# Second layer: output stored by GpSimd with indirect transfers instead of by SyncE

## The reference

```python
xn = layernorm(x)
# attention: a fast-weight recurrence over the leading axis (4 steps here), 16 heads of 64
h = norm(xn) * ln_w + ln_b
q, k, v, beta = split(h @ w_slow);  q, k = sum_norm(elu(q) + 1), sum_norm(elu(k) + 1)
W = 0
for t in range(4):
    W = W + (beta_t * (v_t - W k_t)) k_t^T
    out_t = W q_t
attn = xn + out @ w_out
# feed-forward: 8 experts, the best 2 of each row by softmax(xn @ Wg), their relu nets weighted and summed
x = x + attn + moe(xn)
```

## Time and profile before

| | |
|---|---|
| runs | 1483.12 us median of 2 (1481.14 to 1485.11) |
| the profiled execution, its own time | 1482.89 us |
| its span, first to last instruction | 1481.2 us |
| granted TensorE clock | 0.995 of full speed |
| busy, share of the span | PE 96%, DVE 85%, POOL 65%, ACT 62% |

### The profile page before, as it was taken

How to read it: one execution, slowest core, us unless ns; L and a number is a source line. 1 busy time by engine, 2 the same in 40 slices (tenths; PEclk the granted TensorE clock), 3 DMA queues, 4 the chain that set the end, 5 groups by cost and what they waited for, 6 DMA issues and landing times.

```text
span 1481.2 us, 27229 instructions
## 1 busy us (share of the span) xinstructions
PE 1417.2 (96%) x9282; PEld 914.2 (62%) x9282; DVE 1255.7 (85%) x1966; ACT 916.9 (62%) x1862; POOL 968.5 (65%) x756
## 2 busy tenths in 40 slices
PE   8989999999999999999999998889999999999998
PEld 6755556555555565565655555456667676776767
DVE  7587888788877888888888777479999999999997
ACT  3456666666666667666666675557665675657562
POOL 5144555546555456455555554549999999999895
PEclk9999999999999999999999999999999999999999
DMA  8059777877787778777777778400000000000000
GB/s 189 1 129 217 173 172 179 185 170 175 174 185 173 172 173 186 172 168 178 181 181 166 178 177 199 102 1 1 0 9 8 1 8 1 8 8 1 8 1 15
DMA packets 77140, 163.98 MB, mean 111 GB/s; under 512 B 31410, under 2 KB 43724, under 8 KB 77004
## 3 DMA queue, kind: packets, MB, share of 16 engines
q1 hardware_dynamic: 77004, 162.24, 47.5%
HBM read 9.08 MB, written 2.10 MB: 8 GB/s over the span
## 4 chain that ended last, share of the span: by engine, by line
PE 81%; DVE 7%; issue 5%; POOL 3%; ACT 2%; SPq 0%; DMA 0%; DVEq 0%; ACTq 0%; POOLq 0%
PE accum L1095 17%; PE both L1030 12%; PE misc L997 9%; PE both L2785 8%; PE flips_all L1030 5%; PE flips_all L2808 4%; PE flips_all L1119 4%; PE misc L1007 4%; PE flips_all L2797 3%; PE flips_all L2845 2%; PE accum L2797 2%; PE accum L2808 2%; ACT big L533 2%; PE flips_all L2831 1%; PE flips_all L968 1%
## 5 line engine op out<-in xcount | busy, mean ns | idle before, releaser
L452 POOL TENSOR_SCALAR big<-big,recip 128x384 f32<-128x384 f32 (+7 forms) x512 | 374.4, 745 | 430.5 <-DVE recip L704 430.5
L712 DVE STREAM_TRANSPOSE big<-big 128x896 f32<-128x896 f32 (+7 forms) x288 | 346.0, 1227 | 17.5 <-POOL big L452 16.8
L533 ACT ACTIVATE big<-both,neg_max 128x1024 f32<-128x1024 f32 (+3 forms) x256 | 243.1, 955 | 162.7 <-DVE neg_max L694 157.5
L1095 PE MATMUL accum<-across,v_sb 128*64 128x256 f32 (+1 forms) x2560 | 272.8, 364 | 22.2 <-issue 21.8
L1095 PEld LDWEIGHTS accum<-across,v_sb 128*64 128x64 f32 x2560 | 187.0, 138 | 137.9 <-issue 82.5
L694 DVE TENSOR_REDUCE neg_max<-both 128x1 f32<-128x1024 f32 (+3 forms) x256 | 248.3, 1011 | 7.6 <-PE both L1035 7.6
L1030 PE MATMUL both<-qk_sb 64*128 64x512 f32 (+3 forms) x1024 | 212.9, 532 | 13.1 <-issue 8.2
L533 ACT ACTIVATE big<-flips_all,neg_max 128x128 f32<-128x128 f32 (+3 forms) x256 | 131.6, 525 | 102.7 <-DMA across<-big 59.8
L2785 PE MATMUL both<-slow_sb,h_T 128*128 128x512 f32 x384 | 181.2, 599 | 7.9 <-DVE xnT L2298 4.4
L1594 POOL TENSOR_TENSOR prod<-xnT,qs 128x1024 f32<-128x1024 f32 (+3 forms) x32 | 180.2, 5638 | 11.1 <-DVE qs L2298 11.1
L1030 PEld LDWEIGHTS both<-qk_sb 64*128 64x128 f32 x1024 | 94.1, 186 | 117.9 <-issue 117.9
(11 more groups left out here) (224 smaller groups left out, 2404.9 us busy)
## 6 DMA issues: line engine op xcount, KB each, us to landing
across<-big SPq DMA_DIRECT2D x1024, 144.0 KB, 3.1
out<-x SPq DMA_DIRECT2D x8, 256.0 KB, 2.3
x<-in_L_attn_x SPq DMA_DIRECT2D x3, 512.0 KB, 5.5
slow_sb<-in_L_attn_w_slow SPq DMA_DIRECT2D x3, 512.0 KB, 7.1
w_qk<-in_L_attn_qkv_w SPq DMA_DIRECT2D x2, 512.0 KB, 6.3
xn<-in_L_ffn_W SPq DMA_DIRECT2D x1, 1024.0 KB
x<-in_L_attn_x SPq DMA_DIRECT2D x2, 256.0 KB, 3.0
qs<-in_L_attn_qkv_w SPq DMA_DIRECT2D x1, 512.0 KB, 6.0
```

The source lines that it names most:

```text
L452: pool.tensor_scalar(part, part, recip[:, u % 2, SLOTS.index(row), h:h + 1], 0.0, ALU.mult, ALU.add).then_inc(scaled, 1)
L533: last = act.activation(probs_of(row, h).rearrange("p b j k -> p j b k"), scores_of(row, h).rearrange("p (j b k) -> p j b k", b=MOVES, k=3 ...
L712: dve.transpose(part, part).then_inc(turned[group_of(row)], 1)
L1095: last = pe.matmul(dst, lhsT=values_of(u, j, h), rhs=keys_of(g, rows[n:n + 2], j, h), start=j == 0, stop=j == rows[n + 1])
```

## The change

GpSimd gets a function `store(t)`: with the same waits as SP had it issues four indirect transfers, one for each s, of 128 rows of 512 bytes each. The rows' numbers come from a table `index` that GpSimd makes once by `iota`, between `key_products(0, 2)` and `query_products(0, 2)`. The calls stand in GpSimd's written order: `store(0)` after `sums(2, 2)`, `store(1)` after `sums(3, 2)`, `store(2)` after `row3_high(4)`, `store(3)` after `row3_high(5)`, `store(4)` after `row2(6)`, and `store(5)`, `store(6)`, `store(7)` after its last instruction, `row2(7)`. SP only waits for the end.

```diff
+        index = sb("index", [P, B * ROWS], I32)
...
-        joined, stored = sem("joined"), sem("stored")
-        out_v = out.rearrange("s (t p) e -> t p s e", p=P)
+        joined, stored, index_made = sem("joined"), sem("stored"), sem("index_made")
+        out_v = out.rearrange("s n e -> (s n) e")
...
             last_move(UNITS - 1, 1)
-            for t in range(ROWS):
-                for k, use in latest(given, t, [("expert", e) for e in range(X)] + [("join",)]):
-                    sp.wait_ge(place_kept[k], use)
-                sp.dma_start(out_v[at_of(t)], rows_of(t)).then_inc(stored, 16)
-            sp.wait_ge(stored, 16 * ROWS)
+            sp.wait_ge(stored, 16 * ROWS * B)
...
+            def store(t):
+                if t == 0:
+                    pool.wait_ge(index_made, 1)
+                for k, use in latest(given, t, [("expert", e) for e in range(X)] + [("join",)]):
+                    pool.wait_ge(place_kept[k], use)
+                for s in range(B):
+                    at = ROWS * s + at_of(t)
+                    pool.indirect_dma_start(out_v, bass.IndirectOffsetOnAxis(ap=index[:, at:at + 1], axis=0), row_of(t, s), None
+                                            ).then_inc(stored, 16)
...
             pool.wait_ge(*all_added)
+            pool.iota(index[:], pattern=[[P, B * ROWS]], base=0, channel_multiplier=1).then_inc(index_made, 1)
             query_products(0, 2)
...
             sums(2, 2)
+            store(0)
             query_products(3, 0)
...
             sums(3, 2)
+            store(1)
             query_products(4, 0)
...
             row3_high(4)
+            store(2)
             query_products(5, 0)
...
             row3_high(5)
+            store(3)
             query_products(6, 0)
...
             row2(6)
+            store(4)
             query_products(7, 0)
...
             row2(7)
+            store(5)
+            store(6)
+            store(7)
```

## The result

The changed kernel takes 1513.6 us, the median of two runs (1513.01 to 1514.19), against 1483.12 before: 1.022 times, interval 1.018 to 1.026. Run again on another chip it took 1514.96 us (four runs) against 1481.33. The forecast was 1509.0 us. The kernel is slower beyond doubt; whether by more than 2% the interval leaves open. The direction and most of the size came out as worked out, by single steps that partly didn't.

What follows compares the result with a forecast made beforehand. PE, DVE and POOL were taken as full in the second layer, POOL just on time. Issues at 1.34 us each, 24c - 6.1 = 32.2 - 6.1 = +26.1 us on 1482.89, gave 1509.0 us; range 1487 to 1548.

Steps and rivals of the forecast that it cites:

- What bounds it: In the second layer PE, DVE and POOL are all full, and POOL is on time but not early.
- S: Time from the end of `sums(2, 2)` on POOL to the end of POOL's last product; forecast 21.8 us longer.
- The iota, the waits, SP's removal: Iota hidden in a POOL wait, counted 0; no store waits in its new place; removing SP's issues gives nothing before the end.
- C: Time from the end of POOL's last product to the start of DVE's last addition; forecast -0.25 us.
- T: Time from the end of DVE's last addition to the end of the span; forecast +4.6 us.
- c: Time one indirect transfer's issue holds POOL's queue; taken as 1.34 us, with ends 0.20 and 2.93.
- What is in hand: Lateness taken up after the first store: 2.81 and 2.23 us in POOL's idle times, 0.03 and 0.22 near the end; 5.3 us.
- The stores behind `row2(7)`: `store(5)` and `store(6)` after POOL's last instruction take 10.7 us and fit into the 14.4 us before the last addition ends.
- The tail: After the last addition, `store(7)` is bare: four issues, then the last 64 KB land; +4.6 us.
- Dear issue: Rival: each issue on POOL waits for a DVE instruction and costs 2.56 us; 1544.3 us; chance 0.25.
- Handed over: Rival: POOL passes each transfer on and goes on at once, 0.20 us an issue; time stays 1482.9 us; chance 0.10.
- Made good: Rival: an issue costs 1.34 us but the lateness is made up, leaving only +4.6 us at the end; 1487.5 us; chance 0.08.

Runs made afterwards that it cites:

- eight, stream on SyncE: Against the changed kernel, stores 0 to 4 went back to SyncE while 5, 6 and 7 stayed on GpSimd; 1492.95 us, ratio 1.0076.
- twelve, `store(4)` moved: Against the changed kernel, `store(4)` moved from behind `row2(6)` to behind `row2(7)`, in front of `store(5)`; 1517.29 us, ratio 1.0234.
- twelve, alone: Against the changed kernel, SyncE stored tiles 0 to 3 and 7, GpSimd tiles 4 to 6 in twelve indirect issues after `row2(7)`; 1492.42 us.

## Why the prediction was right or wrong

**What bounds it: right.** POOL is full and just on time in the second layer, and work put there comes out at the end nearly whole. The arithmetic in place of the issues is the proof: it moves no byte, and it brings S up by the same 23.2 us as the stores in the run beside it.

**The iota, the waits, SP's removal: right.** The iota takes 0.17 us, inside a wait for DVE. No store but the last waited for the sums of its tile. Giving the last three stores back to SP changed C and T alone, giving it the first five changed S and little else.

**c: slightly high.** 1.34 us was predicted, 1.26 measured (0.96 and 0.30 of gap), so 20c was 25.1 us and not 26.8. Choosing between POOL's powers of 4 and 8 numbers turned out well, though nothing shows that POOL does such work. The Trainium skill's "DMA: Bandwidth & Descriptors", section Specifications, gives about 1 us to the first byte when GpSimd issues; the estimate by that figure was +17.9 us. The busy part of an issue, 0.96 us, lies near it, but the queue is held for the gap as well, and the total shows that the pitch is what counts.

**What is in hand: the step that failed.** The prediction took 2.81 us off for the idle time at 1209 us, because PE "is hardly late then". It came 2.52 us long and gave 0.29. The trace of the changed kernel shows why. In the timeline of DVE, then of ACT, then of PE, between the first store and that point:

```profile
1184.78 2.29 DVE L2354 TENSOR_REDUCE misc<-prod 128x32 f32<-128x2048 f32 x1 [2.34 <-POOL prod L1591]
...
1207.01 1.22 DVE L2314 SCALAR_TENSOR_TENSOR xnT<-both,e_buf 128x1024 f32<-128x1024 f32 x1 [2.51 <-POOL prod L1591]
```

```profile
1208.32 1.65 ACT L1825 ACTIVATE nrm<-x,shift,rstd 128x128 f32<-128x128 f32 x4 [4.05 <-POOL x L1569]
```

```profile
1208.29 1.98 PE L2801 MATMUL both<-slow_sb,h_T 128*128 128x512 f32 x4 [1.30 <-DVE xnT L2314]
...
1212.15 0.66 PE L2847 MATMUL flips_all<-ident,terms 128*128 128x128 f32 x4 [1.88 <-ACT small L1785]
```

DVE waits for POOL's products at 1184 and at 1207, and PE for that DVE instruction at 1208. ACT waits 4.05 us for POOL's residual, 0.20 us in the kernel before, and PE for ACT at 1212. Corrected for the start, PE is 2.8 us late at the first of its two instructions and 4.9 us at the second. So fifty microseconds after a single block PE is as late as POOL: 4.95 us at POOL's next instruction, against the block's 5.21. An idle time that a follower ends is no reserve once the follower hangs on the engine that is late. For the second idle time I had argued just that, and there the number held: 2.23 us forecast, 4.12 - 1.88 = 2.24 measured. Two new idle times of POOL came in besides, 0.92 us (for DVE; nothing to 0.17 us in four other traces of the same stream) and 0.60 us (for ACT, in each of those too). So 0.29 + 2.24 - 0.92 - 0.60 = 1.0 us is taken up in POOL's idle times, and 25.1 - 23.9 = 1.2 in S (1.9 in the repeated run), where 5.0 were forecast. That is the largest error, 3.9 us.

**The stores behind `row2(7)`: the step that missed a cost.** "8c = 10.7 us fit" is true of POOL's own time, yet C went up by 2.5 us where the last 0.25 us in hand should have shortened it. In the changed kernel's timelines PE and DVE have holes there that nobody's result ends:

```profile
1493.30 1.61 PE L2847 MATMUL flips_all<-ident,terms 128*128 128x128 f32 x13
1495.14 0.52 PE L2847 MATMUL flips_all<-ident,terms 128*128 128x128 f32 x3 [0.22 <-issue]
...
1496.52 0.38 PE L2847 MATMUL flips_all<-ident,terms 128*128 128x128 f32 x2 [0.87 <-issue]
1497.26 0.38 PE L2847 MATMUL flips_all<-ident,terms 128*128 128x128 f32 x2 [0.36 <-issue]
1497.96 1.52 PE L2847 MATMUL flips_all<-ident,terms 128*128 128x128 f32 x12 [0.32 <-issue]
```

```profile
1495.12 1.13 DVE L2341 SCALAR_TENSOR_TENSOR x<-flips_all,score,x 128x128 f32<-128x128 f32 x4 [1.96 <-remote]
...
1498.22 0.69 DVE L2250 COPY outs_T<-flips_all 128x512 f32<-128x512 f32 x1 [1.98 <-remote]
```

The experiments tie them to indirect issues in close succession: C is 19.0 us with none beside it or with plain ones, 20.8 to 21.5 with eight, 27.8 to 29.4 with twelve, 19.0 to 19.4 with pauses. The traces also say when these holes come. The table has, in us, how long after a row's first issue the first of them begins, and then the times at which the row's last issue ends and DVE's held copy starts:

| | first hole | last issue ends | DVE's copy starts |
|---|---|---|---|
| eight, stream on SyncE | 7.7 | 1474.45 | 1476.10 |
| eight, changed kernel | 6.7 | 1496.34 | 1498.22 |
| twelve, `store(4)` moved | 6.7 | 1495.86 | 1498.28 |
| twelve, alone | 7.7 | 1479.42 | 1481.48 |

The holes so begin late in the row and end soon after it. By this reading of four traces, which no further run tested, C grows faster than the count because every issue past that point holds the others for its whole time. Where the stream is that of before, the row of twelve ends 5.0 us later than the row of eight, the last copies start 5.0 (ACT) and 5.4 us (DVE) later, and the slower matmuls behind them add the other 2.0 of the 7.0 us in C. It also fits the pauses, since a block of four takes 5 us. By which way the issues reach PE, DVE and ACT stays open. It isn't a result that the engines wait for. Nor are the transfers a jam: in the trace of the twelve alone, from 1472 to 1482 us, the only queue that moves anything is that of the stores (packets, MB, share of 16 engines), so no instructions were being fetched by the queue that otherwise shows them:

```profile
q0 software_dynamic: 224, 0.46, 13.4%
```

Whether it is the supply of instructions by another way, or the semaphores' signals, wasn't tried.

**The tail: 0.6 us short.** 4c - 0.8 = +4.6 was forecast, +5.2 measured. DVE's last addition ends at 1502.55 + 0.69 = 1503.24:

```profile
1502.55 0.69 DVE L2412 TENSOR_TENSOR x<-accum,x 128x512 f32<-128x512 f32 x1 [3.63 <-PE accum L2861]
```

The first issue starts 1.57 us later, at 1504.81, where SP's started 0.09 us after it. The four take 4.75 us to 1509.56, with the smaller c, and the last bytes 1.75 to the end. The step took over SP's 0.09 us for the time from the release to the first issue.

**Together.** Terms forecast and measured in us: S 26.8 - 5.0 = 21.8, measured 23.9; C -0.25, measured +2.5; T +4.6, measured +5.2. The forecast's sum is 26.1, the measured one 31.6, less the start's 1.5 it is the span's 30.1. In the single terms the errors are -1.7 (c), +3.9 (what is in hand), +2.7 (C) and +0.6 (tail). That 1509.0 lies within 5 us of 1513.6 is therefore partly luck: c taken too high and the earlier start hid 3.2 of the 7.2 us that the other terms lacked. The prediction also gave "within 2%" more than even odds, 0.57; the measured ratio is 1.022, on the other side, and its interval reaches over the line.

**The rivals.** *Dear issue* is out: c is 1.26, and DVE's `keep` takes 1190 to 1226 ns in all 32 cases, as in the earlier trace rows. "SBUF — State Buffer", section SBUF: two separate sides, of the Trainium skill warns that DVE, while it runs in its two-port mode, keeps GpSimd from writing the lists of its transfers. The trace shows nothing of it here, all 32 issues lying within 954 to 1217 ns; no row says whether DVE was in that mode. *Handed over* is out, since c is nearly five times its threshold; the plain transfer of a tile, at 0.75 to 0.98 us, comes nearer to it and isn't it either. *Made good* is out: S kept 23.9 of 25.1 us.

## What to carry to other kernels

Read an engine's room in the stretch where the work is put, and price a transfer by the time that its issue holds the queue it stands in: here 1.26 us for each indirect issue against 0.37 us in an idle queue. An idle time of the late engine is a reserve only if the one who ends it doesn't itself wait, by one or two steps, for that engine; follow that chain before taking it off. And don't gather many indirect issues of GpSimd beside the last work of the others: spread them, or use plain transfers where the rows are regular.

## What the runs showed of the hardware

- An indirect transfer of 128 rows of 512 bytes holds POOL's queue for 0.96 us and 0.30 us of gap, the first of a block for up to 1.22 us. A plain one of 64 KB holds it for 0.54 us, a plain one of 256 KB for 0.75 to 0.98 us.
- Eight indirect issues in a row delayed the end of the other engines' work by 1.7 to 2.5 us, twelve by 8.7 to 10.4 us; twelve plain ones, over in 6.6 us, by 0.0, and twelve in fours with 5 us between them by 0.0. The holes began 6.7 to 7.7 us after the row's first issue, and DVE worked again 1.7 to 2.4 us after the end of its last one.
- Waiting for a result, POOL started its first indirect issue 1.57 or 1.58 us after it in five kernels, and 0.81 us after it where the stream's stores were on SyncE, for a reason that no run shows; a plain issue of 256 KB started after 0.86 us. Behind work of its own it started after 0.13 to 0.19 us.
- After a long stall, with PE busy 1.07 us of 5, PE's granted clock was 0.50 and 16 matmuls took 3.62 instead of 1.95 us. A shorter wait shows too: after PE had waited 4.3 us for POOL the clock in the changed kernel was 0.89 and then 0.95, in stretches with the same columns as above:

```profile
1240.00:1250.00 10.00, 5.71 (x20) 2.69 (x19) 8.13 (x12) 2.79 (x4) 9.84 (x5) 0.89 0.00 1
1250.00:1300.00 50.00, 49.98 (x263) 34.60 (x263) 43.59 (x78) 31.42 (x49) 48.17 (x12) 0.95 0.00 1
```
